# A two-layer sequence kernel: VectorE's order of scan inputs, node rows and second norm, and the place of the attention sum

## The reference, cut to what matters

```python
x = L0_attn_x
xn = _layernorm(x)
x = x + _L0_attn_ref(xn, ...) + _L0_ffn_ref(xn, ...)   # gated linear scan; top-1 of 8 experts
xn = _layernorm(x)
x = x + _L1_attn_ref(xn, ...) + _L1_ffn_ref(xn, ...)   # log-linear attention; recurrent cell
```

## Time and profile before

| what | value |
|---|---|
| median of 3 runs | 1239.69 us (1239.32 to 1242.14) |
| profiled execution | 1243.28 us, span 1241.1 us |
| mean granted TensorE clock | 0.955 |
| TensorE busy | 1094.8 us (88%) |
| VectorE busy | 1002.7 us (81%) |
| ScalarE busy | 698.2 us (56%) |
| GpSimd busy | 310.4 us (25%) |

### The profile page before, as it was taken

One profiled execution on the slowest core, in us unless ns is written; L12 is line 12 of the kernel. 1 busy time (PEld: TensorE's weight loads), 2 busy tenths in 40 slices (PEclk: granted clock), 3 DMA queues, 4 the chain that ended last, 5 costly groups with the idle time before them and its releaser, 6 DMA issues.

```text
span 1241.1 us, 17991 instructions
## 1 busy us (share of the span) xinstructions
PE 1094.8 (88%) x5756; PEld 672.9 (54%) x5756; DVE 1002.7 (81%) x2141; ACT 698.2 (56%) x1366; POOL 310.4 (25%) x197
## 2 busy tenths in 40 slices
PE   5799989998998989999898999999898998989882
PEld 3455636555564655556465555646555564655641
DVE  4688796978979697896979789697978969797667
ACT  4382845738375573837557383655828375573661
POOL 0040220504114050411405041140504114050283
PEclk9799989899999999899999999989999999999885
DMA  3000000000000000000000000000000000002126
GB/s 130 9 9 4 6 17 9 17 8 0 17 8 17 8 17 8 0 17 8 17 8 17 8 0 17 8 17 8 17 8 0 17 8 17 8 17 69 50 94 203
DMA packets 32562, 28.64 MB, mean 23 GB/s; under 512 B 1568, under 2 KB 26144, under 8 KB 32288
## 3 DMA queue, kind: packets, MB, share of 16 engines
q1 hardware_dynamic: 32544, 28.42, 6.9%
HBM read 16.09 MB, written 12.32 MB: 23 GB/s over the span
## 4 chain that ended last, share of the span: by engine, by line
PE 53%; DVE 34%; issue 9%; ACT 2%; DMA 1%; DVEq 0%; SPq 0%; POOLq 0%; POOL 0%; ACTq 0%
DVE ms L1248 6%; PE p L462 5%; PE p L581 4%; PE p L619 3%; DVE skip L1080 3%; PE p L544 3%; PE p L477 3%; PE p L479 2%; PE p L478 2%; PE p L556 2%; PE p L570 2%; DVE pair L1321 2%; PE p L433 2%; DVE nodesT L1257 2%; PE p L424 2%
## 5 line engine op out<-in xcount | busy, mean ns | idle before, releaser
L1509 POOL TENSOR_TENSOR pair<-pair,cgt 128x2048 f32<-128x2048 f32 x16 | 58.4, 3648 | 799.8 <-DVE pair L1308 799.8
L852 ACT ACTIVATE gx<-p 128x512 f32<-128x512 f32 x256 | 143.6, 592 | 14.9 <-PE p L479 9.3
L477 PE MATMUL p<-x1Th,Gl 128*128 128x512 f32 x256 | 120.0, 469 | 4.0 <-ACT gx L852 4.0
L812 ACT ACTIVATE gelu<-p,bias_u 128x512 f32<-128x512 f32 x32 | 22.0, 687 | 153.6 <-PE p L424 153.6
L479 PE MATMUL p<-x1Th,Gh 128*128 128x512 f32 x256 | 101.9, 398 | 0.0
L478 PE MATMUL p<-x1Tl,Gh 128*128 128x512 f32 x256 | 101.6, 397 | 0.0
L1522 POOL TENSOR_TENSOR vp<-vdw,beta 128x384 f32<-128x384 f32 (+3 forms) x80 | 80.8, 1043 | 56.0 <-DVE beta L1300 56.0
L544 PE MATMUL p<-gx,x1T 128*32 128x512 f32 x512 | 74.1, 653 | 15.2 <-DVE pair L1325 14.4
L581 PEld LDWEIGHTS p<-vbd,pair 128*128 128x128 f32 x512 | 62.8, 193 | 43.0 <-issue 34.4
L1248 DVE TENSOR_TENSOR ms<-lam,K 128x64 f32<-128x64 f32 (+4 forms) x80 | 84.5, 1132 | 0.0
L394 PE MATMUL p<-xnT,MC 128*128 128x512 f32 x64 | 38.0, 680 | 46.5 <-DVE y L1153 46.5
(11 more groups left out here) (239 smaller groups left out, 2707.1 us busy)
## 6 DMA issues: line engine op xcount, KB each, us to landing
xin<-in_x SPq DMA_DIRECT2D x16, 256.0 KB, 2.8
hx_scratch<-vdw SPq DMA_DIRECT2D x16, 256.0 KB, 2.5
res_scratch<-res SPq DMA_DIRECT2D x15, 256.0 KB, 2.0
W<-in_weights SPq DMA_DIRECT2D x1, 1477.5 KB, 9.0
gx<-hx_scratch SPq DMA_DIRECT2D x5, 256.0 KB, 3.9
out<-gx SPq DMA_DIRECT2D x5, 256.0 KB, 2.7
gx<-in_weights SPq DMA_DIRECT2D x1, 1216.0 KB, 11.4
GT<-hx_scratch SPq DMA_DIRECT2D x4, 256.0 KB, 4.0
```

Of the source, the lines that this page charges most:

```text
L477: pe.matmul(head_bank(h)[:, :], tile(Gl, h), x1Th[:, :], start=True, stop=False)
L852: act.activation(tile(gx, h, T), head_bank(h)[:, :], ACT.Copy).then_inc(R["gx_copied"], 1)
```

## The change

VectorE's order becomes: level weights, statistics of the second norm, scan inputs, node products, transposition of the nodes, second norm, scans. The attention sum `ob` is no longer a part of `rs` but the tile `skip` itself, so `attention_out` adds in place and `norm2` normalises in place; `attention_out` waits for the copy into `skip`. ScalarE's `left_halves` waits for the attention sum and for the cell (which still uses a part of `rs`) in place of `norm2`.

```diff
-        yt, ytT, ob = rs[:, 0:T], rs[:, T:2 * T], rs[:, 2 * T:3 * T]
+        yt, ytT, ob = rs[:, 0:T], rs[:, T:2 * T], skip
...
                 if later(i):
-                    act.wait_ge(R["n_ready"], i)
+                    act.wait_ge(R["ob_ready"], i)
+                    act.wait_ge(R["c_ready"], B if isinstance(i, int) else i)
...
             def attention_out(i):
                 dve.wait_ge(R["wo_ps"], i + 1)
-                if later(i):
-                    dve.wait_ge(R["n_ready"], i)
+                dve.wait_ge(R["skip_ready"], i + 1)
...
                     if later(i):
                         stats2(i - 1)
+                if j is not None:
+                    scan_inputs(j)
+                if i is not None:
                     node_lams(i)
-                if j is not None:
-                    scan_inputs(j)
-                if i is not None:
+                    node_rows(i)
                     if later(i):
                         norm2(i - 1)
-                    node_rows(i)
                 if j is not None:
                     scans(j)
```

More of the change, by code:

```diff
@@ L1423, in stages @@
                         stats2(i - 1)
-                    node_lams(i)
                 if j is not None:
@@ L1427, in stages @@
                 if i is not None:
+                    node_lams(i)
+                    node_rows(i)
                     if later(i):
                         norm2(i - 1)
-                    node_rows(i)
                 if j is not None:
```

## The result

The changed kernel takes 1275.45 us (median of four runs, 1270.95 to 1279.66) where the kernel before takes 1240.91 beside it (1239.32 to 1242.17): a ratio of 1.0278, 95% interval 1.0239 to 1.0318. It is **slower**, by 2.8%. Its profiled execution took 1274.43 us with a span of 1272.2; before it was 1243.3 and 1241.1, so the two traces differ by 31.1 us, a little less than the medians (34.5).

The account below looks back on a forecast made before the run. VectorE's unbroken line up to the first pair weights was taken as the bound, then TensorE. 2.22 us over 13 stages (28.9) plus stages 0 and 1 gave +31 us on the 1239.7 median: 1270.5 us, range 1248 to 1288.

Parts of the forecast that it names:

- Sum over the skip, left halves: Attention sum written to the skip tile, and ScalarE's left halves starting 0.91 us earlier: both worth nothing.
- The stall moves to the node products: VectorE beside GpSimd's own-level product: the stall leaves norm2 for the last node product, which still ends at 600.18.
- the list at the end of the prediction: Signs expected in the changed profile, such as the largest node product over 4 us and norm2's first instruction at 0.33.
- Finish meets the scans: GpSimd's finish starts with VectorE's scans and they take turns: 0.97 us lost a stage, bounds 0.45 to 1.3.
- Residual and copy meet the routing: GpSimd's residual sum and skip copy delay VectorE's expert-choice comparisons: 1.25 us a stage, bounds 0 to 1.9.
- rival 1: Only the scans pay, the routing does not wait for GpSimd: 1254.6 us; chance 0.17.
- The sum of a stage: Stages 2 to 14: 0.97 + 1.25 = 2.22 us lost each, 28.9 over 13 stages; VectorE's loss moves the end one to one.
- TensorE's wait ahead of scores 1: TensorE's wait for the first pair weights grows from 1.29 to about 2.8 us.
- rival 2: TensorE's clock dips behind the new wait ahead of scores 1; some 9 more stages pay 2.2 us: 1290 us; chance 0.10.
- Stage 0, stage 1 and the ends: Stages outside 2 to 14: stage 0 loses 2.9 us, stage 1 ends 0.6 earlier, stage 15 changes by 0.
- The term for the transposition: VectorE's transposition, then norm2 without stall in 1.10 us: scans begin at 603.6 in place of 603.18.

Follow-up runs that it names:

- the third experiment: Changed kernel with GpSimd's residual sum and skip copy held until the end of the routing; 1263.05 us, ratio 1.0193.
- the changed kernel with filler: Changed kernel with repeated TensorE left-half products, the third done three times and the fourth twice; 1271.15 us, ratio 1.0247.
- the second experiment: Changed kernel with scan inputs back behind the node products, transposition still ahead of the second norm; 1230.03 us, ratio 0.9912.
- 72.39 with filler: Changed kernel with second norm ahead of the transposition again, third and fourth left-half products each done three times; 1247.92 us, ratio 1.0064.

## Why the prediction was right

The forecast was 1270.5 us (its terms add up to 31.2, which on 1239.7 gives 1270.9) and the measured time 1275.45. Sign and size came out, and in the loop stages the mechanism; the terms for the clock, for stage 1 and for stage 15 did not. Step by step:

- **Sum over the skip, left halves: nothing.** Shown by the run of that part alone, ratio 1.0006.
- **The stall moves to the node products.** It does: 0.31 us for norm2, 4.24 for a node product. It sits in the 512-column product, not in the largest, as the list at the end of the prediction had it, because GpSimd got to its long product one VectorE instruction sooner. The node products end 39.23 us into the stage, where the own-level product ended 38.99 into it before; predicted was the same time.
- **Finish meets the scans, 0.97 us.** The second scan takes 2.25 us (predicted some 2.2), and the first pair weights are ready 1.13 us later in the stage (48.09 to 49.23). The run that holds finish back gains only 0.35 us at the stage's end, because finish meets a pair weight there instead, so it doesn't contradict the 0.97.
- **Residual and copy meet the routing, 1.25 us.** The two comparisons take 1.17 + 0.58 in place of 0.28 + 0.28: 1.19 us. Holding the residual back gives 1.1 us a stage. So these instructions on 32 partitions wait as those on 128 do. The prediction had no row for this, and rival 1 hung on it; the rival falls. The Trainium skill, SBUF — State Buffer, section "Who interferes with whom", names the two engines and the two SBUF inputs and makes no exception for few partitions; these rows agree.
- **The sum of a stage, 2.22 us.** The scores that TensorE starts at 621.36 and now at 712.53 come 2.31 us later in the stage (60.17 to 62.48), and a stage without the early dip is 74.28 us long, 2.30 more (predicted 74.2). That VectorE's loss moves the end one to one holds.
- **TensorE's wait ahead of scores 1, near 2.8 us.** Measured 1.26 in the stage shown. There a dip of 3.4 us from 692.2 stretches the node matrices (1.58 us in place of 1.1) and what follows them into that wait, and costs nothing by that; where no dip comes ahead of it the wait is 2.89 us, as the third experiment shows.
- **The clock, rival 2.** It came about in part, and its price was misread. The prediction put the 2.2 us of a stage of 74.19 down to the dip behind the 2.97 us wait; 1.7 of them belong to the early dip of the same stage, which its rows leave out, and 0.5 to that one. Early dips became six in place of three (5.1 us lost), and the others no longer cost anything (1.5 us gained): 3.6 us net, the larger part of the 4.6 us by which the 13 stages lie above their forecast (33.5 against 28.9). The prediction looked for the dip at the new wait ahead of scores 1. What costs here comes behind the 1.98 us wait at the stage's start, which the kernel before had too and which the change doesn't touch; at the wait ahead of scores 1 it came in two of the experiments (residual held back, and the changed kernel with filler), not in the changed kernel itself.
- **Stage 0, stage 1 and the ends.** 4.1 us for 2.9 predicted (a dip from 91.5 to 98.3 lies in stage 0), 0.85 for -0.6 (an early dip lies in stage 1, where the kernel before has none). The tail is 4.7 us shorter for 0 predicted. The prediction looked at the left halves of stage 15 and not at its transposition: there are no scan inputs ahead of the node products in that stage, so the order is that of the second experiment. The transposition starts 42.3 us into the stage in place of 46.7, because the four norm2 instructions, which took 4.54 us ahead of it, now follow it with 2.19, and the first pair weights are begun 2.4 us earlier. The other 2.3 us come where the kernel before has a dip of 6.8 us more (from 1186.3); no run separates the two. That the total of the traces comes out at 31.1, just as forecast, is thus partly luck: 33.5 us in the stages against 28.9, and the ends against it.

The term for the transposition was right inside this change and would be wrong alone. Laid out as a square (with the sum over the skip in all four): neither half 1241.16 us, transposition first 1230.03, scan inputs first 1277.17, both 1275.45. The scan inputs ahead of the node products are the harmful half, for two reasons that the runs separate: 0.4 us a stage at full clock (72.39 with filler), and 2.7 us of dips (75.09). Beside the transposition the first reason grows to 2.8 us (74.29 against 71.52). With either place of the scan inputs finish then meets the scans and the residual the routing; the difference is in the node products, which take 7.8 us together in the changed kernel (681.51 to 689.28) and 5.1 in the second experiment, while the stall of norm2 is gone in both.

**Open** is what makes a given stage dip. The same 1.98 us wait is followed by a dip in one stage and not in the next, of the same kernel and the same instructions, and filling another wait changed how often (from 13 stages to six in one kernel, from five to eight in another). The length of one wait doesn't decide it. In stages 2 to 14 of all these traces every dip begins inside a wait of TensorE or at most 1.6 us behind one.

## What to carry to other kernels

A long GpSimd instruction needs VectorE work beside it that doesn't contend with it, here operations that read PSUM and the transposition, 3.5 us of it beside an instruction that needs 3.6; spent anywhere else, the stall returns in whatever comes next. When a step is moved, follow what it releases on the other engine, through its DMA too (norm2, finish, 2.25 us later the residual), and see which VectorE work it lands on. A wait of TensorE is paid a second time where the granted clock falls behind it, so fill the waits with real work, and all of them: with one filled, dips stayed at another, and in two kernels came or became more there; only with the last one filled did the time fall to 1194.72 us. And look for every dip of a stage before putting a price on one of them.

## What the runs showed of the hardware that I had not expected

- Short instructions with two SBUF operands on 32 partitions wait in full for GpSimd: 1.17 us in place of 0.28.
- A wait of TensorE of 1.8 to 2.0 us can be followed by 3.4 or 6.8 us at half the clock (granted 0.50). The early dip cost 1.7 us in every kernel that has stages with and without it; one near the middle of a stage cost between nothing (74.29 with and without, where it took up a wait that came anyway) and 2.1 us (72.52 against 70.43). Eight more TensorE instructions in a stage, repeated products, made the kernel 29 us faster (1277.17 to 1247.92).
- With the same waits of 2.95 us for the scan inputs and of 1.98 us at the stage's start, a kernel dipped in two of its 13 stages (1230.03 us), and in eight once two waits elsewhere in the stage were gone (1229.65 us).
